# Cross attention of the last two sequences: its elementwise work shared between GpSimd and VectorE, with operands copied into PSUM

## The reference

```
xn = layernorm(x);  N, L, H, Dh = 4, 256, 16, 8
q = (xn  @ Wq.T + bq).reshape(N, L, H, Dh).transpose(0, 2, 1, 3)
k = (ctx @ Wk.T + bk).reshape(N, L, H, Dh).transpose(0, 2, 1, 3)
v = (ctx @ Wv.T + bv).reshape(N, L, H, Dh).transpose(0, 2, 1, 3)
energy = einsum('nhld,ngld->nlhg', q, k)
attn   = softmax(energy / sqrt(128), axis=3)
out    = einsum('nlhg,ngld->nhld', attn, v)   # then layernorm, affine, @ Wo.T + bo
x = x + out
```

## Time and profile before

| | |
|---|---|
| time, median of 3 runs | 1174.65 us (1174.62 to 1174.73) |
| profiled execution: time / span from first to last instruction | 1175.91 / 1174.1 us |
| busy over the span: PE, DVE, ACT, POOL | 73%, 51%, 30%, 29% |
| mean granted TensorE clock | 0.834 of full |
| end of the last self-attention unit on PE | 979.36 us |
| last xw of cross attention read by DVE | 1040.08 us |

### The profile page before, as it was taken

How to read it: one execution, slowest core, us unless ns; L and a number is a source line. 1 busy time by engine, 2 the same in 40 slices (tenths; PEclk the granted TensorE clock), 3 DMA queues, 4 the chain that set the end, 5 groups by cost and what they waited for, 6 DMA issues and landing times. The chain is left out here.

```text
span 1174.1 us, 15927 instructions
## 1 busy us (share of the span) xinstructions
PE 854.0 (73%) x5969; PEld 617.9 (53%) x5969; DVE 596.9 (51%) x1400; ACT 352.5 (30%) x685; POOL 339.9 (29%) x324
## 2 busy tenths in 40 slices
PE   5964887945664465798879327999999997157994
PEld 2541454633442453576645215567878776134994
DVE  2655843214599814775654466755336444342222
ACT  1110674220122012165446212344343332011331
POOL 1363101223088422222310210000034347625131
PEclk9985997975697677799889657789999998558897
DMA  9202200640000025063560000000000000004584
GB/s 391 92 1 80 68 4 1 181 116 1 19 0 1 1 44 127 22 133 77 132 175 4 1 1 0 1 1 2 1 2 1 3 1 1 0 1 169 190 274 151
DMA packets 44677, 72.43 MB, mean 62 GB/s; under 512 B 4817, under 2 KB 36737, under 8 KB 43033
## 3 DMA queue, kind: packets, MB, share of 16 engines
q1 hardware_dynamic: 38921, 65.72, 18.9%
q0 software_dynamic: 1728, 3.59, 0.9%
q10 hardware_dynamic: 3952, 2.10, 0.7%
HBM read 58.65 MB, written 15.89 MB: 63 GB/s over the span
## 5 line engine op out<-in xcount | busy, mean ns | idle before, releaser
L842 DVE TENSOR_REDUCE space<-PS 128x2 f32<-128x512 f32 x128 | 83.5, 687 | 41.7 <-PE PS L651 41.3
L2392 DVE TENSOR_REDUCE space<-PS 128x2 f32<-128x512 f32 x64 | 44.0, 688 | 91.9 <-PE PS L2134 91.7
L826 ACT ACTIVATE annex<-PS 128x384 f32<-128x384 f32 (+1 forms) x128 | 66.9, 545 | 54.1 <-PE PS L660 24.3
L2146 PE MATMUL PS<-space 64*128 64x256 f32 x256 | 80.9, 409 | 0.0
L2163 PEld LDWEIGHTS PS<-space 128*128 128x128 f32 x512 | 63.5, 195 | 20.9 <-issue 20.0
L2163 PE MATMUL PS<-space 128*128 128x65 f32 x512 | 72.3, 286 | 0.2 <-ACT space L2249 0.2
L1913 POOL TENSOR_TENSOR space<-space 128x1536 f32<-128x1536 f32 x16 | 54.6, 3441 | 37.7 <-ACT space L1786 31.4
L1133 PE MATMUL PS<-space 128*128 128x128 f32 x444 | 57.3, 284 | 8.6 <-DVE space L1268 2.6
L2249 ACT ACTIVATE space<-PS 128x512 f32<-128x512 f32 x64 | 38.2, 597 | 75.6 <-PE PS L2147 75.5
L1133 PEld LDWEIGHTS PS<-space 128*128 128x128 f32 x444 | 53.6, 197 | 11.3 <-issue 6.1
L1268 DVE TENSOR_TENSOR space<-PS,space 128x512 f32<-128x512 f32 (+1 forms) x28 | 19.2, 687 | 72.3 <-ACT space L1195 67.1
(11 more groups left out here) (488 smaller groups left out, 2241.1 us busy)
## 6 DMA issues: line engine op xcount, KB each, us to landing
space<-in_e_l_ffn SPq DMA_DIRECT2D x22, 768.0 KB
space<-in_e_l_ffn SPq DMA_DIRECT2D x23, 192.0 KB, 2.7
l_ffn_sorted<-in_slots SPq DMA_DIRECT2D x2, 1584.0 KB, 25.5
space<-l_attn_scratch_k SPq DMA_DIRECT2D x8, 384.0 KB
space<-l_ffn_sorted SPq DMA_DIRECT2D x10, 264.0 KB, 5.1
weights<-in_w_l_xattn SPq DMA_DIRECT2D x1, 2504.0 KB, 15.3
weights<-in_w_l_attn SPq DMA_DIRECT2D x1, 2124.0 KB, 12.0
space<-l_xattn_scratch_q SPq DMA_DIRECT2D x4, 512.0 KB, 3.5
```

Source lines behind the costliest of these rows:

```text
L826: nc.scalar.activation(P[:, u % 8, 0:keys], PS[:, 3 + u % 2, 0:keys], ACT.Exp).then_inc(exp_done, 1)
L842: nc.vector.tensor_reduce(m[:, :, at_h], PS[:, u % 3, :].rearrange("p (c k) -> p c k", c=2), AX_X, ALU.max).then_inc(max_done, 1)
L2146: nc.tensor.matmul(out, kk[:, 128 * kc:128 * kc + 128], q, start=True, stop=False)
L2392: nc.vector.tensor_reduce(MX[:, b % 2, :, h], PS[:, a % 2, :].rearrange("p (c k) -> p c k", c=2), AX_X, ALU.max).then_inc(max_done, 1)
```

## The change

It applies to sequences 2 and 3 only (`SHARED`; the value is a PSUM bank). ACT copies tile 1's queries and values a second time, from the shared bank into PSUM banks 0 and 1 (sequence 2) or 3 and 4 (sequence 3), which self attention has left, ahead of its usual copies; they are counted on a new semaphore `beside`. POOL's `products` and `values` do tile 0 only. DVE does tile 1: PR[1] = queries in PSUM x keys in SBUF, and weights in SBUF x values in PSUM. The maxima go to PSUM, and DVE subtracts them itself (POOL's `shift` falls away). In the planner `sum1` and `sum0` move to the step of `products` and `weigh1` and `weigh0` to the step of `values`, in this order: DVE issues products, sum1, sum0 at one step, and dens, values, weigh1, weigh0 at another. That is steps 83 and 89 for sequence 2, steps 99 and 105 for sequence 3; `shift` (the maximum and the subtraction) stays at 87 and 103, `scale` at 94 and 110.

```diff
+    SHARED = {B - 2: 0, B - 1: 3}
...
         for i, what in ((1, "products"), (3, "sum0"), (5, "sum1"), (5, "shift"), (6, "expx"), (7, "dens"), (7, "values"),
                         (9, "weigh0"), (12, "weigh1"), (12, "scale"), (13, "out"), (14, "normedo")):
+            if b in SHARED and what[:-1] in ("sum", "weigh"):
+                continue
             piece(f + i, what, b)
+            if b in SHARED and what in ("products", "values"):
+                piece(f + i, "sum1" if what == "products" else "weigh1", b)
+                piece(f + i, "sum0" if what == "products" else "weigh0", b)
...
                 dst = {"xk": KX, "xv": VX, "xq": QX}[kind][:, b % 2]
+                if b in SHARED and kind != "xk":
+                    nc.scalar.copy(PS[:, SHARED[b] + (kind != "xq"), 0:128], out[:, 128:256]).then_inc(beside, 1)
                 ins = nc.scalar.copy(dst, out[:, 0:256].rearrange("p (t d) -> p t d", t=2))
...
+            elif what == "products":
+                dve.wait_ge(beside, 2 * (b - B + 2) + 2)
+                dve.wait_ge(*emptied("xk", b, 0))
+                queries = PS[:, SHARED[b], 0:128].rearrange("p (h d) -> p h d", d=8)
+                own(nc.vector.tensor_tensor(PR[:, 1, :].rearrange("p (h g d) -> p h g d", h=16, g=16), bcast(queries, 2, 16),
+                                            bcast(KX[:, b % 2, 1, :].rearrange("p (h d) -> p h d", d=8), 1, 16), ALU.mult))
+                own.settle()
+            elif what == "values":
+                dve.wait_ge(exped, b + 1)
+                dve.wait_ge(beside, 2 * (b - B + 2) + 2)
+                values = PS[:, SHARED[b] + 1, 0:128].rearrange("p (h d) -> p h d", d=8)
+                own(nc.vector.tensor_tensor(PR[:, 1, :].rearrange("p (h d g) -> p h d g", h=16, d=8),
+                                            bcast(e[:, 1, :].rearrange("p (h g) -> p h g", h=16), 2, 8),
+                                            bcast(values.rearrange("p g d -> p d g"), 1, 16), ALU.mult))
+                own.settle()
+            elif what == "shift":
+                m, top = e.rearrange("p t (h g) -> p (t h) g", g=16), PS[:, SHARED[b], 0:32]
+                dve.wait_ge(summed, 2 * b + 2)
+                own(nc.vector.tensor_reduce(top, m, AX_X, ALU.max))
+                own.settle()
+                nc.vector.tensor_tensor(m, m, bcast(top, 2, 16), ALU.subtract).then_inc(shifted, 1)
...
-                for t in range(2):
+                for t in range(2 if b not in SHARED else 1):
```

More of the change, by code:

```diff
@@ L1964, in feedforward_attentions @@
     fills, bias_ready, bout_psum, bout_ready = (sem(x) for x in ("_fills", "_bias", "_bout_psum", "_bout"))
+    beside = sem("_beside")
     xn_ready, xnx_ready, on_ready = sem("_xn"), sem("_xnx"), sem("_on")
@@ L2041, in emptied, with products_before @@
         return free[i % 2], i // 2 + 1
-    tiles_of = lambda b: (2 * b, 2 * b + 1)
+    def products_before(b):
+        return sum(2 if x in SHARED else 4 for x in range(b))
     def tensor(pe, own):
@@ L2225, in leave @@
                 if kind == "xv" and b >= 2:
-                    act.wait_ge(multiplied, 4 * (b - 2) + 4)
+                    act.wait_ge(multiplied, products_before(b - 1))
                 if kind in ("xk", "xq") and b >= 2:
-                    act.wait_ge(multiplied, 4 * (b - 2) + 2)
+                    act.wait_ge(multiplied, products_before(b - 1) - 2)
                 dst = {"xk": KX, "xv": VX, "xq": QX}[kind][:, b % 2]
+                if b in SHARED and kind != "xk":
+                    nc.scalar.copy(PS[:, SHARED[b] + (kind != "xq"), 0:128], out[:, 128:256]).then_inc(beside, 1)
                 ins = nc.scalar.copy(dst, out[:, 0:256].rearrange("p (t d) -> p t d", t=2))
@@ L2341, in cross @@
                 centred("cross", b, xt(b), xnt(b), c.moments, 2 * b, xnx_ready)
+            elif what == "products":
[19 more added lines that the diff above has]
+                nc.vector.tensor_tensor(m, m, bcast(top, 2, 16), ALU.subtract).then_inc(shifted, 1)
             elif what in ("sum0", "sum1"):
                 t = int(what[3])
-                dve.wait_ge(multiplied, 4 * b + t + 1)
+                if b not in SHARED or t == 0:
+                    dve.wait_ge(multiplied, products_before(b) + t + 1)
                 nc.vector.tensor_reduce(e[:, t, :], PR[:, t, :].rearrange("p (m d) -> p m d", d=8), AX_X, ALU.add).then_inc(summed, 1)
-                if t == 1:
+                if t == 1 and b not in SHARED:
                     dve.wait_ge(summed, 2 * b + 2)
@@ L2355, in cross @@
                 t = int(what[5])
-                dve.wait_ge(multiplied, 4 * b + 2 + t + 1)
+                if b not in SHARED:
+                    dve.wait_ge(multiplied, products_before(b) + 2 + t + 1)
+                elif t == 0:
+                    dve.wait_ge(multiplied, products_before(b) + 2)
                 nc.vector.tensor_reduce(O[:, b % 2, t, :], PR[:, t, :].rearrange("p (m g) -> p m g", g=16), AX_X, ALU.add).then_inc(summed2, 1)
@@ L2427, in vector @@
                 feedforward(*p)
-            for p in pieces(step, "cross", "normedx", "sum0", "sum1", "dens", "weigh0", "weigh1", "out", "normedo"):
-                cross(*p)
+            for p in pieces(step, "cross", "normedx", "products", "sum0", "sum1", "shift", "dens", "values", "weigh0", "weigh1", "out", "normedo"):
+                if p[1] in SHARED or p[0] not in ("products", "shift", "values"):
+                    cross(*p)
             if step == FROM + 9:
@@ L2483, in gpsimd @@
             for p in pieces(step, "products", "shift", "values", "scale"):
-                cross(*p)
+                if p[1] not in SHARED or p[0] != "shift":
+                    cross(*p)
     def sync(sp, own):
```

## The result

| | before | after |
|---|---|---|
| time, median (range, runs) | 1174.63 us (1168.86 to 1174.73, 4) | 1161.07 us (1152.63 to 1163.47, 4) |
| ratio, 95% interval | | 0.9892 [0.9856, 0.9929] |
| profiled execution: time / span | 1175.91 / 1174.1 | 1163.04 / 1161.2 |
| mean granted TensorE clock | 0.834 | 0.836 |
| last self-attention unit on PE ends | 979.36 | 983.35 |

What follows compares the result with a forecast made beforehand. It took the POOL, DVE and ACT chain in sequence 3's cross attention as the bound: 8.02 us gained there less 0.57 lost in sequence 2, 7.45 off 1174.65, gives 1167.2 us; 8-in-10 range 1164.2 to 1171.5.

Steps and rivals of the forecast that it cites:

- Rival B: DVE's strided PSUM read of the values is slow: 1168.1 us at POOL's ratio, 1171.4 at double cost; chance 0.20.
- Rival C: DVE waits out POOL's instruction in products and values: 5.9 us slower together, 1180.5 us; chance 0.05.
- The scheme for sequence 2: Sequence 2: weigh0 ends earlier, but the o of step 90 queues behind it on DVE; 0.57 us lost at half clock.
- which clock?: Self attention's last projection on PE, at 994: expected at the lower level, 1.2 GHz, after a wait for the bank.
- XN to S: Sequence 3, from DVE's start on the normalised input to the start of POOL's products: gain 0 forecast.
- S to E: Sequence 3, from the start of POOL's products to the end of the exponential: gain 3.00 us forecast.
- E to weigh0: Sequence 3, from the end of the exponential to the end of weigh0: gain 5.02 us forecast.
- stretch: From PE's last self-attention unit to the end of DVE's reading of the last xw: 7.45 us less forecast.
- Rival A: Self attention's last projection runs at full clock, 2.4 GHz: 9.82 us off, 1164.8 us; chance 0.20.
- Rival D: Sequence 3's gain is lost later to PE or a transfer: full loss 1174.7 us; 0.10 together with small losses.
- about 1 us either way: Behind the last xw: the clock may rise at other places, changing the time by about 1 us.
- tail: From DVE's reading of the last xw to the end of the span; forecast to move only about 1 us either way.

Runs made afterwards that it cites:

- two_sbuf_inputs: The changed kernel with DVE reading tile 1's queries and values from SBUF, ACT's copies to PSUM kept: 1175.35 us, ratio to before 1.0045.
- weigh_after_o: The changed kernel with weigh1 and weigh0 one step later, so DVE reads the o of step 90 first: 1160.21 us, ratio to before 0.9900.
- before_look: The kernel before, unaltered, for a second profile: 1165.5 us in one run.
- products_only: The changed kernel with only products and subtraction shared with DVE, values and weigh sums as before: 1164.07 us, ratio to before 0.9961.
- values_only: The changed kernel with only the values shared with DVE, products, maxima and subtraction as before: 1163.70 us, ratio to before 0.9948.
- all_behind_o: Against reordered_warm: sequence 2's dens, values and weigh sums behind reading o, 12 useless matmuls instead of 22 ahead of xT: 1155.99 us, ratio to before 0.9840.
- weigh_after_o_warm: weigh_after_o plus 22 useless matmuls on PE ahead of sequence 3's transpose: 1159.35 us, ratio to before 0.9885.
- after_again: The changed kernel once more, unaltered: 1156.34 us, ratio to before 0.9899.
- after_beside: The changed kernel again, unaltered, on one chip with a repeat of weigh_after_o: 1158.97 us, ratio to before 0.9879.
- reordered_warm: weigh_after_o_warm with expx one step later, sum0 four steps later, and 12 more useless matmuls ahead of sequence 3's xo: 1157.67 us, ratio to before 0.9866.

## Why the prediction was wrong in size

**What held.** The costs of the operations: products 2.28 us as forecast, values 2.23 for 2.28, POOL's tiles at 4.48 and 5.42 beside them. Rival B fell: reading PSUM at a step of 8 elements costs nothing. Rival C fell for this kernel, because each DVE operation has one input in PSUM; two_sbuf_inputs shows that it would otherwise have decided. That agrees with the Trainium skill's "SBUF — State Buffer", section "Who interferes with whom". The nearness of C's price, 5.9 for 6.5, was in part luck. The scheme for sequence 2 held too: both weigh sums done 13.0 us after the last unit instead of 18.9, the o of step 90 stuck behind weigh0, half clock for the next o (3.75 us), `out` 19.77 us after the last unit where it had been 19.61. All the gain of sequence 2 was lost in DVE's queue, and weigh_after_o shows it by removing that wait.

**The step that failed.** "Call S the start of POOL's products, 1006.38 before. DVE's products stand at step 99, behind xw of sequence 2 at step 98, which DVE reads at 1007.63 for 0.42, that is S + 1.67." That carried the timing of before into the new order: PE at half clock for xT, xo, xq and xw, and nothing gained between XN and S. The prediction asked "which clock?" of the one projection at 994 and answered rightly, but did not ask it again of the next work on PE. The delayed o keeps PE busy until 1004.8 instead of leaving it idle, so xT comes 2.03 us after PE's last work, not 6.47, and the clock is at its upper level. DVE has read xw by S + 0.68 (1009.78 + 0.42), not by S + 1.67. The missing gain by part: XN to S 1.01 us, though ACT's extra copy of 0.25 now lies in it; S to E 1.22, of it 1.1 because DVE's products start at S + 0.60 and not at S + 1.70; E to weigh0 0.25; sequence 2 0.41. Less 0.01 behind weigh0 that is 2.88, and 10.33 - 7.45 = 2.88. Some 2.1 of it is the clock at xT and the projections, the term that was mis-sized; the rest are small surpluses in the sum. Another 2 us, also the clock's, came behind the stretch, as shown below.

What shows the clock as cause: with PE idle for 6.47, 6.49 and 7.65 us before xT (before, before_look, products_only) XN to S is 4.49 to 4.66 us; with 3.06 and 3.07 (weigh_after_o twice) 4.50 and 4.45; with 2.03 to 2.34 (after three times, values_only, two_sbuf_inputs) about 3.5; and with idle time taken up by useless matmuls (all_behind_o) 3.48. In one and the same order of the work, weigh_after_o and weigh_after_o_warm, filling the gap alone takes the first projections from 1.19 to 0.67 us.

**Rival A** gave nearly the measured size of gain, 9.82, for the wrong reason: the projection of self attention at full clock, which did not happen. **Rival D** looked behind the last xw, but for a loss. The prediction's "about 1 us either way" for the clock there was the second thing too small: the tail is 133.6 and 130.4 us in two profiles of before and 127.0, 127.9 and 126.1 in three of after, in unchanged code.

**What lies behind the stretch.** The stretch accounts for 10.3 us, a ratio of 1 - 10.33 / 1174.65 = 0.9912. Each of the three intervals of after holds it (the last only just), but the three ratios themselves lie 0.0013 to 0.0033 lower, 1.5 to 3.9 us. Some 2 us of that stand in the first 18 us of the tail, where the same instructions run at another granted clock: the 16 matmuls of L1091 take 3.53 us before and 1.90 after, which is 1.6 of the 2, and DVE waits for them.

PE and then DVE of before, in order of time, behind the last xw:

```profile
1054.59 3.53 PE L1091 MATMUL PS<-space,const_tile 128*128 128x56 f32 x16
```

```profile
1058.16 0.17 DVE L1230 TENSOR_SCALAR space<-PS 128x7 f32<-128x7 f32 x1 [2.49 <-PE PS L1091]
```

and of after:

```profile
1047.74 1.90 PE L1091 MATMUL PS<-space,const_tile 128*128 128x56 f32 x16
```

```profile
1049.68 0.17 DVE L1230 TENSOR_SCALAR space<-PS 128x7 f32<-128x7 f32 x1 [0.71 <-PE PS L1091]
```

DVE's L1230 starts 17.7 us after the last xw before (17.8 in before_look) and 15.5 after (15.8 in after_again, 15.7 in after_beside). This part repeats with the kernel. From the last unit to L1230 the change takes 12.3 to 12.6 us off, a ratio of about 0.989, which is what the times show. It also answers for much of the 3.3 us of weigh_after_o: its L1230 starts at 17.8 and 17.7, as in before, so that up to there it is only 1.0 to 1.2 us ahead of after.

**What stays open.** Why the clock is low at L1091 in some kernels was not found. The clock at xT does not decide it: L1091 takes 3.53 us in two_sbuf_inputs and weigh_after_o_warm too, whose xT was fast. Nor does L1091 settle the rest of the tail: products_only has the same 3.53 us and a start of L1230 at 17.6, and yet the shortest tail of all, 125.7 us. That rest also differs between profiles of one kernel (133.6 and 130.4 for before), and whether any of it follows the kernel needs many profiles of each, which were not made.

## What to carry to other kernels

When a change lets one engine's work slip, ask for PE's clock not only at the work that slips but at the next work behind it: a delay that fills a gap on PE gives back part of its cost (here 1.3 us of 4.6 in the stretch, by weigh_after_o against after). GpSimd and VectorE can share elementwise work if one of VectorE's inputs is copied into PSUM first (0.25 us a copy on ScalarE here, against 1.4 to 6.0 us more for each VectorE operation without it). Time a local change by the stretch that it touches, which repeats to 0.1 us in the profile, and not by one pair of runs, which differ by 10; but follow it on behind its end, where the clock can add or take back 2 us in every execution.

## What the runs showed of the hardware

- VectorE's instructions with both inputs in SBUF waited out GpSimd's, in four cases of four: they ended 2.14 and 2.15 us (products) and 3.70 and 3.71 us (values) after GpSimd's end.
- The same values, at a step of 8 float32 elements, cost 2.23 us from PSUM for 2048 elements, and from SBUF an estimated 3.70, if VectorE's work began when GpSimd's ended.
- Identical instructions in an unchanged part of the kernel (the tail) took 126.1 to 127.9 us in three profiles of one kernel and 130.4 and 133.6 in two of another. Some 2 us of that are PE's granted clock up to L1230 (L1091, 1.90 against 3.53 us).
- Some 5 us of useless matmuls kept the granted clock up, but a matmul behind them on PE's queue waits for all of them: xT started 1.67 us after its input was ready instead of 0.15, which used up the 1.3 us that the clock gave (weigh_after_o_warm), and 3.07 us after it in reordered_warm.
